# One row of a depthwise convolution a tap earlier, a norm chain over a whole chunk, and three merged ScalarE steps taken apart

## The reference

```
x = x + L0(gn(x))
x = x + L1(gn(x))

L0: xh = w_in x + b_in                        64 -> 128 channels
    kernels = kg_w2 relu(kg_w1 mean(xh))      nine taps per channel and image
    y = depthwise 3x3 convolution(xh, kernels)
    y = y * tanh(softplus(y)); out = w_out y  128 -> 64 channels

L1: offset, mask = two 3x3 convolutions of x
    nine taps per pixel: bilinear sample of x at (pixel + tap + offset), times mask
    z = 1x1 convolution of [w_def samples, offset, mask]; out = silu(bn(z))
```

## Time and profile before

| | |
|---|---|
| time of the profiled execution | 5553.13 us |
| its span, first to last instruction | 5551.3 us |
| mean granted TensorE clock | 0.816 of 2.4 GHz |
| VectorE busy | 4482.9 us, 81% |
| TensorE busy | 4454.9 us, 80% |
| GpSimd busy | 4029.9 us, 73% |
| ScalarE busy | 2568.2 us, 46% |

### The profile page before, as it was taken

One profiled execution on the slowest core, in us unless ns is written; L12 is line 12 of the kernel. 1 busy time (PEld: TensorE's weight loads), 2 busy tenths in 40 slices (PEclk: granted clock), 3 DMA queues, 4 the chain that ended last, 5 costly groups with the idle time before them and its releaser, 6 DMA issues.

```text
span 5551.3 us, 46053 instructions
## 1 busy us (share of the span) xinstructions
PE 4454.9 (80%) x14762; PEld 1992.6 (36%) x14762; DVE 4482.9 (81%) x5298; ACT 2568.2 (46%) x3568; POOL 4029.9 (73%) x4243
## 2 busy tenths in 40 slices
PE   7688787888878788787888878878788787878784
PEld 3233333433333333343333433333343333333331
DVE  6978969788797987978889697897978878788765
ACT  4444444544445454454444444454454444544321
POOL 2777777777777777677777777777777777777776
PEclk8788878788787888878888788887878878788886
DMA  4334353443534434344343443535344353433433
GB/s 118 107 122 133 106 144 101 133 123 111 140 101 131 123 115 137 100 132 123 116 135 102 135 120 118 133 102 146 105 133 122 106 144 103 132 115 113 122 107 100
DMA packets 279695, 667.35 MB, mean 120 GB/s; under 512 B 76447, under 2 KB 116762, under 8 KB 277210
## 3 DMA queue, kind: packets, MB, share of 16 engines
q0 software_dynamic: 203328, 555.49, 33.3%
q1 hardware_dynamic: 76128, 108.93, 7.8%
HBM read 610.00 MB, written 54.12 MB: 120 GB/s over the span
## 4 chain that ended last, share of the span: by engine, by line
PE 42%; DVE 29%; ACT 13%; issue 10%; POOL 6%; DMA 0%; DVEq 0%; ACTq 0%; POOLq 0%; SPq 0%
PE yo_ps L775 8%; DVE gat L1372 7%; PE conv_ps L643 7%; PE z_ps L695 7%; POOL gat L504 6%; DVE pairs L1351 6%; PE tap_ps L775 5%; DVE conv_ps L1242 5%; PE tap_ps L689 4%; DVE hat_s L1399 4%; PE conv_ps L568 3%; PE xh_ps L755 2%; PE yo_ps L658 2%; DVE stat L1265 2%; DVE xb L1263 1%
## 5 line engine op out<-in xcount | busy, mean ns | idle before, releaser
L504 POOL DMA_INDIRECT gat<-patch_table,ixu x4236 | 4021.6, 949 | 1507.3 <-issue 1253.5
L1372 DVE TENSOR_TENSOR gat<-gat,wgt_ps 128x1024 f32<-128x1024 f32 x1059 | 1278.6, 1215 | 324.1 <-DMA gat<-patch_table,ixu 316.2
L1351 DVE TENSOR_REDUCE pairs<-gat 128x256 f32<-128x1024 f32 x1024 | 1240.5, 1211 | 0.0
L775 PE MATMUL yo_ps<-hat_s,hat_image 128*128 128x512 f32 x1860 | 972.0, 675 | 12.9 <-issue 12.9
L689 PE MATMUL tap_ps<-ident,pairs 128*128 128x128 f32 x2048 | 422.5, 342 | 689.5 <-DVE pairs L1351 689.4
L775 PE MATMUL tap_ps<-hat_s,hat_image 128*128 128x512 f32 x1860 | 925.0, 648 | 0.0
L1042 ACT ACTIVATE val<-tap_ps 128x512 f32<-128x512 f32 x512 | 304.5, 595 | 1280.5 <-PE tap_ps L689 1280.3
L689 PEld LDWEIGHTS tap_ps<-ident,pairs 128*128 128x128 f32 x2048 | 291.5, 173 | 1020.1 <-DVE pairs L1351 842.2
L1242 DVE SCALAR_TENSOR_TENSOR conv_ps<-xh,kb,conv_ps 128x1024 f32<-128x1024 f32 x480 | 618.0, 1287 | 12.7
L775 PEld LDWEIGHTS yo_ps<-hat_s,hat_image 128*128 128x128 f32 x1860 | 387.1, 218 | 586.7 <-issue 585.2
L775 PEld LDWEIGHTS tap_ps<-hat_s,hat_image 128*128 128x128 f32 x1860 | 381.2, 215 | 443.5 <-issue 427.0
(11 more groups left out here) (228 smaller groups left out, 4842.3 us busy)
## 6 DMA issues: line engine op xcount, KB each, us to landing
gat<-patch_table,ixu POOLq DMA_INDIRECT x4236, 2.7
xb<-in_x SPq DMA_DIRECT2D x31, 1024.0 KB, 10.9
patch_table<-rec SPq DMA_DIRECT2D x120, 256.0 KB, 2.4
hat_image<-patch_table SPq DMA_DIRECT2D x144, 128.0 KB
out<-n_z SPq DMA_DIRECT2D x128, 128.0 KB, 2.3
patch_table<-np SPq DMA_DIRECT2D x2, 1072.5 KB
patch_table<-gat SPq DMA_DIRECT2D x8, 256.0 KB, 2.2
patch_table<-rec SPq DMA_DIRECT2D x16, 96.0 KB
```

Of the source, the lines that this page charges most:

```text
L504: pool.indirect_dma_start(gat[:, k, t * 2 * REC:(t + 1) * 2 * REC], None, table_rows, bass.IndirectOffsetOnAxis(ixu[:, i, k, t:t + 1], 0)) ...
L775: m = pe.matmul(hat_sums[t % 2][:, :], hat_image[:, q // NCH % 2, i, t, :], hat_s[:, i, :], start=(i == 0), stop=(i == HI - 1))
L1351: dve.tensor_reduce(total, gat[:, k, :].rearrange("p (t x c h) -> p t c x h", t=TILES, x=2, h=2), mybir.AxisListType.XY, ALU.add).then_inc ...
L1372: dve.tensor_tensor(patch, patch, wk.rearrange("p (n h) -> p n h", h=2).unsqueeze(2).to_broadcast([128, TILES * 2, C, 2]), ALU.mult).then_ ...
```

## The change

- In chunks 0 to 3 the three convolution rows move one tap forward (in chunk 1 to 3 from 3, 4, 5 to 2, 3, 4; in chunk 0 from 2, 3, 5 to 1, 2, 4), and exp, ln, tanh and the residual with them. `project` stays behind the last tap.
- In chunk 6 the chain from the variance to the kernels is spread out; its last VectorE step, `kernels`, moves to chunk 7. TensorE's `hidden` no longer waits for it.
- ScalarE's `hidden` becomes `norms` and `evict`, and its part of `hat_y` becomes `hat_round`, each with a place of its own.
- In the last image all eight chunks compute the ninth tap.

```diff
-PLAN_BLOCK0 = ((2, "residual"), (3, "convolve 0"), (4, "convolve 1"), (5, "convolve 2"), (6, "exp"), (7, "ln"), (8, "tanh"), (8, "finish"), (KK, "project"))
+PLAN_BLOCK0 = ((1, "residual"), (2, "convolve 0"), (3, "convolve 1"), (4, "convolve 2"), (5, "exp"), (6, "ln"), (7, "tanh"), (8, "finish"), (KK, "project"))
...
-PLAN_NEXT_HAT = ((0, "hat_y"), (3, "hat_part"), (4, "hat_x"), (6, "hat_mask"), (8, "hat_weigh"), (KK, "hat_select"))
+PLAN_NEXT_HAT = ((0, "hat_y"), (1, "hat_round"), (3, "hat_part"), (4, "hat_x"), (6, "hat_mask"), (8, "hat_weigh"), (KK, "hat_select"))
...
-    return q < B * NCH and q % NCH in (HATS if q >= NCH else HATS0)
+    return q < B * NCH and (q >= (B - 1) * NCH or q % NCH in (HATS if q >= NCH else HATS0))
...
                     pe.wait_ge(n0_done, q + 2)
-                    if n > 1 and s == 0 and j == 0:
-                        pe.wait_ge(kernel_dve, n * KERNEL_STEPS + 8)
                     pe.wait_ge(xh_done, q + 1)
...
-            def hidden(n, s):
+            def evict(n, s):
...
-                if n > 0:
-                    if s == 0:
-                        act.wait_ge(kernel_dve, n * KERNEL_STEPS + 7)
-                    for j in range(2):
-                        act.wait_ge(xh_mm, n * NCH + s * 2 + (j + 1))
-                        act.activation(n0[C:, j, :], xb[C:, n % 2, span(s * 2 + j)], ACT.Identity, bias=mr0[C:, 2:3],
-                                       scale=mr0[C:, 1:2]).then_inc(n0_done, 1)
...
+            def norms(n, s):
+
+                if s == 0:
+                    act.wait_ge(kernel_dve, n * KERNEL_STEPS + 7)
+                for j in range(2):
+                    act.wait_ge(xh_mm, n * NCH + s * 2 + (j + 1))
+                    act.activation(n0[C:, j, :], xb[C:, n % 2, span(s * 2 + j)], ACT.Identity, bias=mr0[C:, 2:3],
+                                   scale=mr0[C:, 1:2]).then_inc(n0_done, 1)
```

More of the change, by code:

```diff
@@ L52 @@
 ROUND = 12582912.0
-PLAN_FIRST = ((2, "convolve 0"), (3, "convolve 1"), (5, "convolve 2"), (6, "exp"), (7, "ln"), (8, "tanh"), (KK, "project"))
-PLAN_BLOCK0 = ((2, "residual"), (3, "convolve 0"), (4, "convolve 1"), (5, "convolve 2"), (6, "exp"), (7, "ln"), (8, "tanh"), (8, "finish"), (KK, "project"))
+PLAN_FIRST = ((1, "convolve 0"), (2, "convolve 1"), (4, "convolve 2"), (5, "exp"), (6, "ln"), (7, "tanh"), (KK, "project"))
+PLAN_BLOCK0 = ((1, "residual"), (2, "convolve 0"), (3, "convolve 1"), (4, "convolve 2"), (5, "exp"), (6, "ln"), (7, "tanh"), (8, "finish"), (KK, "project"))
 PLAN_START = (
@@ L62 @@
 )
-PLAN_NORM = ((2, "residual"), (4, "group_mean"), (5, "group_var"), (6, "normalise"), (8, "finish"))
+PLAN_NORM = ((1, "residual"), (4, "group_mean"), (5, "group_var"), (6, "normalise"), (8, "finish"))
 PLAN_PREPARE = (
@@ L66 @@
      (5, "to_table 2"), (6, "x_stats 2"), (6, "to_table 3"), (7, "to_pixels 1"), (8, "to_table 4"), (8, "finish"), (KK, "x_stats 3")),
[L67 to L70, removed]
+    ((1, "x_mean"), (1, "offsets 2"), (2, "to_table 5"), (3, "x_var"), (3, "points 0"), (4, "offsets 3"), (4, "to_pixels 2"), (4, "to_table 6"),
+     (5, "points 1"), (5, "x_norm"), (6, "hidden_units"), (6, "to_table 7"), (6, "to_pixels 3"), (7, "points 2"), (7, "kernel_taps"), (7, "norms 0"),
+     (8, "hidden 0"), (8, "finish"), (KK, "evict 0"), (KK, "norms 1")),
+    ((0, "hidden 1"), (1, "points 3"), (1, "evict 1"), (1, "norms 2"), (2, "kernels"), (2, "next_indices"), (2, "hidden 2"), (3, "points 4"),
+     (3, "evict 2"), (3, "norms 3"), (4, "hidden 3"), (5, "evict 3"), (5, "points 5"), (8, "finish")),
 )
@@ L1091, in _ @@
             act.wait_ge(cleared, 2)
-            hidden(0, 0)
+            evict(0, 0)
             x_norm(0)
-            hidden(0, 1)
+            evict(0, 1)
             hidden_units(0)
             for s in range(2, NCH // 2):
-                hidden(0, s)
+                evict(0, s)
             for s in range(NCH // 2):
@@ L1119, in _ @@
             for s in range(NCH // 2):
-                hidden(1, s)
+                norms(1, s)
+                evict(1, s)
             def image(b, more, further):
@@ L1132, in image @@
                 steps["hat_rows"] = lambda b, g, i: hat_rows(b * NCH + g)
-                steps["hat_y"] = lambda b, g, i: hat_y(b * NCH + g + 1)
+                steps["hat_round"] = lambda b, g, i: hat_y(b * NCH + g + 1)
                 steps["hat_x"] = lambda b, g, i: hat_x(b * NCH + g + 1)
                 if further:
-                    steps["hidden"] = lambda b, g, i: hidden(b + 2, i)
+                    steps["norms"] = lambda b, g, i: norms(b + 2, i)
+                    steps["evict"] = lambda b, g, i: evict(b + 2, i)
                     steps["x_var"] = lambda b, g, i: x_var(b + 2)
```

## The result

The changed kernel takes 5645.28 us (median of four runs, 5640.14 to 5658.55), the kernel before 5551.44 us in the same comparison: 1.0173 times as long, 95% interval 1.0155 to 1.0191, or 94 us more. 5598 us was forecast, 47 us more; the direction and the place were right, the size was half of what came. The profiled execution took 5640.14 us, 87 us more than that of before.

A forecast was written before the change was run, and what follows sets the result against it. The prediction took a loop through VectorE's chunks and GpSimd's gathers as the bound, with GpSimd alone 10.8 us per image below. 14 x (9.4 - 5.3) - 10 = +47 us on 5553.1 us gave 5598 us, range 5560 to 5640 (chance 0.45).

The forecast's parts named there:

- ScalarE's three terms in chunks 6 and 7: Two ScalarE waits gone (-2.8 us), norms and evictions ahead of `hat_part` (+2.9), TensorE's wait for norms gone (-1.9), per image.
- The loop and its floor: Chunks 6 to 3 set each image's 339.3 us; GpSimd's gathers need 328.5 us, so at most 10.8 us can be won.
- Rows, chunks 0 to 3: Third row delays tap 3's corner sum 3.93 us; each chunk 2.3 us longer, +9.4 us per image, bounds -5.0 and +10.9.
- the chain: TensorE in chunks 0 to 3, from pair 1's start to hat product 3's end: priced at 16.7 us.
- Row 6: Image 14's chunk 7, profiled before the change: a chain of 16.30 us behind an idle stretch of 3.85 us.
- The second offset block: TensorE, chunk 6: starts when ScalarE's copy of the first block is there, -3.5 us for all queued behind it.
- The bound of 7.7 us: Most that chunks 6 and 7 could gain: image 14's take 91.0 us against 98.7 us in image 6.
- Last image and the edits at nothing: Last image: 8 gathers fewer in chunks 5 and 6, -10 us; `kernels` in chunk 7 and `hat_round` behind hat lines: nothing.
- The stalls: Rival, chunks 6 and 7: VectorE's 7.4 and 8.8 us waits both vanish, -105 us, some 5446 us; chance 0.17.
- The clock: Rival, chunks 0 to 3: TensorE's clock stays up, chain 13.12 us, -154 us, some 5397 us; chance 0.10.
- No gain in chunks 6 and 7: Rival: ScalarE's longer queue ahead of `hat_part` eats what TensorE wins, +122 us, some 5673 us; chance 0.15.
- The two: Rival: a 7.7 us gain in chunks 6 and 7 cancels the rows' loss with a 16.3 us chain, about -9 us; chance 0.13.

The follow-up runs named there:

- e8: e7 plus matmuls whose result nobody reads, 11 ahead of pair 0 and 22 ahead of pair 1, in chunks 0 to 3: 5425.84 us.
- e1: Kernel before with only the convolution rows, exp, ln, tanh and residual a tap earlier: 5712.46 us, ratio 1.0291.
- e2: Changed kernel with the convolution rows, exp, ln, tanh and residual where they stood before: 5492.80 us, ratio 0.9898.
- e4: Changed kernel plus 22 matmuls whose result nobody reads, ahead of pair 0 and of pair 1 in chunks 0 to 3: 5532.40 us.
- e9: Changed kernel with only the third convolution row back behind tap 3, and ln early: 5442.79 us, ratio 0.9805.
- e7: e2 with ln right behind exp, ahead of ScalarE's copy of pair 2: 5431.28 us, ratio 0.9784.
- e5: Changed kernel with the rows back in their old place in image 0 alone: 5635.49 us, ratio 1.0148.
- e6: Kernel before with only the norm chain stretched over chunk 6 and without TensorE's wait, ScalarE's steps merged: 5489.42 us, ratio 0.9891.
- e10: e2 with ScalarE's rounding back ahead of the hat lines, norms and evictions still apart: 5492.30 us, ratio 0.9894.

## Why the prediction was right in direction and short in size

Two steps of the prediction failed. The rows were put at nothing in image 0, where they cost 15 us by themselves. And ScalarE's three terms in chunks 6 and 7 were put at a gain of 1.8 us per image, where none came; if anything, about 1 us was lost.

**The loop and its floor: right.** Longer chunks in 0 to 3 lengthened every image, and as they became shorter the images came down to GpSimd's floor. It is 330.9 us (`e8`), 2.4 above my 328.5, as the pauses between gathers are a little longer.

**Rows, chunks 0 to 3: the mechanism right, the total right by luck.** Pair 1 was put at 22.28 + 3.93 = 26.2 us and came at 26.12; tanh's wait fell, hat products 2 and 3 became the waits; the clock at pair 1 stayed at 0.50. The term I chose was the chain, 16.7 us as the mean of rows 4 and 6. It took 17.16 us in the chunk shown, and its chunk was 2.7 us longer, what the prediction gave for 17.09. Row 6 was the wrong neighbour: 3.85 us of idle time ahead of pair 1, where the case to price had 5.8. Chunks 1 to 3 grew by 2.9 us each where 2.3 was forecast. Chunk 0, which had the same price, grew by only 0.7 us (in `e1` it became 0.4 shorter); why is not shown. The two errors cancel: chunks 0 to 3 grew by 9.4 us per image, the figure forecast. The 2.0 us that the rows cost in chunks 6 and 7 of `e1` do not come in the changed kernel, whose chunks 6 and 7 are as long as those of `e2` (97.91 and 97.79 us). `e4` shows that the clock, not the number of instructions, makes the chain long, and `e9` against `e7` that the third row makes it late. Tanh's remaining wait of 1.8 us, which I had called small, is in the shadow of the chain: product 3 is waited for right behind it.

**Image 0: counted as nothing, and this failed.** The rows cost 15.1 us there (`e1`); 12.8 of these are the two waits shown with `e5`. In the changed kernel they cost more, 369.7 - 347.4 = 22.3 us against image 0 of `e2`, which the rest of the change had made 9.8 us shorter than before. Part of it is given back in image 1: undoing it gave 10 us (`e5`), at the edge of what can be told.

**Chunks 6 and 7: the largest error, a gain of 5.3 us forecast.** The second offset block moved as said. TensorE and, below, what it waits for, in image 6 after the earlier trace rows:

```profile
2482.42 8.12 PE L642 MATMUL conv_ps<-np,w_om 128*41 128x512 f32 x24 [2.95 <-ACT cat L1002]
```

```profile
2481.65 0.72 ACT L1002 ACTIVATE cat<-cat,half_c 9x512 f32<-9x512 f32 x1
```

It starts as the copy ends. This term, -3.5 us, came as some -4.4 per image with the edit that holds it (`e6`: 62 / 14). The three ScalarE terms failed: -2.8 + 2.9 - 1.9 = -1.8 us was forecast, and about +1.0 came (14 / 14, from `e6` and `e2`). I had let ScalarE's two short waits and TensorE's 1.90 us count in full, although `hat_part` stands behind all of ScalarE's queue, and VectorE waits there longer than before:

```profile
2537.15 0.69 DVE L1386 SCALAR_TENSOR_TENSOR hat_d<-hat_g,xh_ps 128x512 f32<-128x512 f32 x1 [13.72 <-ACT hat_g L1077]
```

Together that is 14 x (1.8 + 1.0 - 0.9) = 27 us of the miss. The copies' starts agree: chunks 6 and 7 of images 1 to 13 went from 101.75 to 98.39 us, -3.4 where -5.3 was forecast. The bound of 7.7 us had been read from image 6, whose 98.7 us are less than the mean.

**Last image and the edits at nothing: right.** -10.0 us came where -10 was forecast; the rounding's place changes nothing (`e10`). That of `kernels` was not tried by itself.

**The rivals.** The stalls did not go whole: the deviation's wait went and the one for the hat lines grew. The clock did not stay up, and this rival's price was wrong too: with the clock up in most chunks (`e4`) the kernel takes 5532 us, not 5397, and 40 us more than without the rows (`e2`). No gain in chunks 6 and 7 was wrong, though the queue that this rival spoke of is the likely place where ScalarE's part went. The two did not cancel.

**The account of the 47 us that were missing.** The forecast gives image 0 of the profiled execution -5.3 us (its chunks 6 and 7), images 1 to 13 4.1 each and image 14 9.4, which is 62.7 for images 1 to 14. Image 0 came at +12.5, 17.8 more; images 1 to 14 came at +85.2, 22.5 more, about what chunks 6 and 7 fell short by. That is 40 us; the other 7 lie between the profiled executions and the medians (5.1 us after, 1.7 before).

## What to carry to other kernels

Before a step is moved forward to end a wait, look at what its engine delivers behind it: here one row of 3.93 us ahead of a corner sum made chunks 1 to 3 2.9 us longer, while the wait for tanh only fell from 3.1 to 1.8 us, and that wait could be shortened by moving one activation on another engine (`e7`). A chain that starts behind an idle stretch is priced from the row with the same idle time ahead of it, not from a mean of rows, and the first image is priced by itself, since steps that are moved forward there can come before their inputs. And a queue's own waits are no gain as long as its last instruction is the one that others stand for.

## What the runs showed of the hardware

In `e4`, 44 more matmuls in chunk 2 of image 5 went with a chunk 3.3 us shorter (43.93 against 47.21 us), with a granted clock behind them of 1.00 and not 0.50; in chunk 1, where the clock was 0.50 in spite of them, it took 47.12 us. In the changed kernel chunks with the same work differed (46.65, 47.21 and 47.50 us for chunks 1 to 3 of image 5) as the clock's rise fell earlier or later into hat product 2, which took 5.45, 6.01 and 6.30 us.
